# Query projections in one earlier slot, the query rows' transfers ahead of the left half's, and a reordered prologue, in a macaron block on one core

## The reference

```python
x = x + 0.5 * ffn(layernorm(x))     # ffn: fft, matmul with a complex w, real part of ifft, + bias
x = x + attn(layernorm(x))          # 16 heads of 8, q/k/v from the LEFT 128 features, then Wo and bo
x = x + 0.5 * ffn(layernorm(x))
# attn: softmax(q @ k.T / 4) @ v per head
```

## Time and profile before

| | us |
|---|---|
| median of 3 runs | 317.19 |
| lowest, highest | 316.79, 319.31 |
| profiled execution, its own time | 320.35 |
| its span | 318.5 |
| busy share of the span: PE, ACT, DVE, POOL | 94%, 81%, 60%, 31% |
| DMA, mean | 157 GB/s |
| granted TensorE clock | 1.000 of full speed |

### The profile page before, as it was taken

One profiled execution on the slowest core, in us unless ns is written; L12 is line 12 of the kernel. 1 busy time (PEld: TensorE's weight loads), 2 busy tenths in 40 slices (PEclk: granted clock), 3 DMA queues, 4 the chain that ended last, 5 costly groups with the idle time before them and its releaser, 6 DMA issues.

```text
span 318.5 us, 8826 instructions
## 1 busy us (share of the span) xinstructions
PE 298.2 (94%) x3445; PEld 113.4 (36%) x3449; DVE 189.6 (60%) x550; ACT 259.3 (81%) x287; POOL 97.7 (31%) x112
## 2 busy tenths in 40 slices
PE   8888899899999999999997999899998999998985
PEld 5644333233333333333332333233332333222333
DVE  1687535758775778477863778367854653360264
ACT  2215989998998989898996989798998999999921
POOL 6734701043604251404504251403500340034014
PEclk9999999999999999999999999999999999999999
DMA  7835572146456364825474363625461564112102
GB/s 202 312 134 196 204 285 115 58 160 240 138 184 221 134 199 141 290 105 200 133 224 176 134 201 117 184 101 199 136 203 66 185 214 165 38 68 66 36 33 68
DMA packets 26564, 49.86 MB, mean 157 GB/s; under 512 B 2065, under 2 KB 14737, under 8 KB 24721
## 3 DMA queue, kind: packets, MB, share of 16 engines
q1 hardware_dynamic: 25824, 48.78, 44.4%
q10 hardware_dynamic: 688, 0.40, 0.7%
HBM read 31.34 MB, written 17.83 MB: 154 GB/s over the span
## 4 chain that ended last, share of the span: by engine, by line
PE 66%; DMA 11%; DVE 10%; issue 6%; ACT 5%; POOL 1%; SPq 1%; PEldq 0%; ACTq 0%; DVEq 0%
PE misc L715 24%; PE ot L823 24%; PE scores L795 12%; DMA QS<-q_scr 9%; ACT probs L665 5%; DMA left_scr<-left_blocks 3%; PE scores L682 2%; DVE left_blocks L963 2%; PE scores L715 1%; PE scores L689 1%; DVE kp L982 1%; DVE lh L954 1%; DVE kp L980 1%; DVE stats L936 1%; DVE VS L1027 1%
## 5 line engine op out<-in xcount | busy, mean ns | idle before, releaser
L665 ACT ACTIVATE probs<-scores 128x1024 f32<-128x1024 f32 x256 | 243.9, 1029 | 25.6 <-PE scores L795 22.7
L823 PE MATMUL ot<-probs,VS 128*32 128x512 f32 x1024 | 134.4, 594 | 3.9 <-ACT probs L665 2.9
L795 PE MATMUL scores<-QS,KS 32*128 32x512 f32 x512 | 64.8, 495 | 5.7 <-DMA QS<-q_scr 5.0
L795 PEld LDWEIGHTS scores<-QS,KS 32*128 32x128 f32 x512 | 24.5, 181 | 112.8 <-ACT probs L665 100.3
L1014 DVE SCALAR_TENSOR_TENSOR x_out<-misc,rstd,x_out 128x256 f32<-128x256 f32 x28 | 13.6, 484 | 48.2 <-PE misc L715 44.8
L823 PEld LDWEIGHTS ot<-probs,VS 128*32 128x32 f32 x1024 | 30.8, 109 | 28.0 <-ACT probs L665 7.1
L558 POOL TENSOR_TENSOR x_out<-x,half_bias 128x512 f32<-128x512 f32 x7 | 9.0, 1290 | 92.4 <-DVE x L1009 92.4
L543 POOL TENSOR_SCALAR veps<-mv 128x4 f32<-128x4 f32 (+1 forms) x25 | 5.7, 227 | 96.4 <-DVE mv L943 96.4
L715 PE MATMUL misc<-half_ffn,xT 128*32 128x256 f32 x448 | 33.1, 387 | 0.0
L715 PE MATMUL misc<-half_ffn,xT_in 128*32 128x256 f32 x400 | 27.9, 385 | 1.8 <-DVE half_ffn L1185 1.3
L545 POOL TENSOR_TENSOR rstd<-veps,power 128x4 f32<-128x4 f32 (+1 forms) x25 | 25.2, 1008 | 2.1
(11 more groups left out here) (126 smaller groups left out, 259.3 us busy)
## 6 DMA issues: line engine op xcount, KB each, us to landing
KS<-k_scr SPq DMA_DIRECT2D x14, 512.0 KB, 4.5
QS<-q_scr SPq DMA_DIRECT2D x14, 512.0 KB, 4.5
x_in<-x SPq DMA_DIRECT2D x8, 512.0 KB, 6.4
xT_in<-x_t SPq DMA_DIRECT2D x8, 512.0 KB, 7.3
k_scr<-kp SPq DMA_DIRECT2D x8, 512.0 KB, 2.8
q_scr<-qp SPq DMA_DIRECT2D x8, 512.0 KB, 3.7
x_scr<-x_blocks SPq DMA_DIRECT2D x7, 512.0 KB, 3.5
xT<-x_scr SPq DMA_DIRECT2D x7, 512.0 KB, 4.5
```

Source lines behind the costliest of these rows:

```text
L665: nc.scalar.activation(probs[u % PRING][:, :, :], scores[u % SRING][:, :, :], ACT.Exp, scale=SCORE_SCALE).then_inc(exp_done, 1)
L795: last = mm(scores[(u + j // 2) % SRING][:, j % 2, :], KS[b % 2][rows, slot, kt * P:(kt + 1) * P].bitcast(F32R), QS[b % 2][rows, slot, :]. ...
L823: last = mm(ot[COL * j:COL * (j + 1), :], VS[b % 2][:, kt, h, :], probs[(u + j // 2) % PRING][:, j % 2, :], start=s % 8 == 0, stop=s % 8 == 7)
```

## The change

In `STEADY` both QT halves move to slot 6 (one left, one right), F1_3 moves from 6 to 7, and V_0 and V_1 stand apart in 8 and 9 (before: QT_0 in 7, QT_1 in 8, both V in 9). DVE's `left_half` goes from slots 8 and 9 to 9 and 10, and ACT's square of the queries from quad 10 to 9. `BEGIN` is mixed anew: KT and QT halves share slots with F1 parts, and V comes in 11 and 12. SP issues both query row loads straight behind the query store, ahead of the left half's two transfers, and the x loads behind an output store. In the prologue all of batch 0's statistics come behind the second fold, POOL's rstd ahead of its bias adds, and batch 1's statistics behind the guard's maxima.

```diff
 STEADY = ...
-          6: [("F1_3a", 2, LEFT), ("F1_3", 2, LEFT)], 7: [("QT_0", 1, LEFT)], 8: [("QT_1", 1, LEFT)],
-          9: [("V_0", 1, RIGHT), ("V_1", 1, LEFT)], 10: ...
+          6: [("QT_0", 1, LEFT), ("QT_1", 1, RIGHT)], 7: [("F1_3a", 2, LEFT), ("F1_3", 2, LEFT)],
+          8: [("V_0", 1, RIGHT)], 9: [("V_1", 1, LEFT)], 10: ...
-BEGIN = {1: [("LT", 1, LEFT)], 2: [("KT_0", 1, LEFT), ("KT_1", 1, RIGHT)], 3: [("QT_0", 1, LEFT), ("QT_1", 1, RIGHT)],
-         4: [("F1_0a", 2, LEFT), ("F1_0", 2, LEFT)], 5: [("F1_1a", 2, LEFT)], 6: [("F1_1", 2, LEFT), ("F1_2a", 2, RIGHT)],
-         7: [("F1_2", 2, RIGHT)], 8: [("F1_3a", 2, LEFT), ("F1_3", 2, LEFT)], 9: [("V_0", 1, RIGHT)],
-         10: [("V_1", 1, LEFT), ("N", 1, RIGHT)]}
+BEGIN = {1: [("LT", 1, LEFT)], 2: [("KT_0", 1, RIGHT), ("F1_0a", 2, LEFT)], 3: [("F1_0", 2, LEFT), ("KT_1", 1, RIGHT)],
+         4: [("F1_1a", 2, LEFT)], 5: [("F1_1", 2, LEFT), ("QT_0", 1, RIGHT)], 6: [("F1_2a", 2, LEFT)],
+         7: [("F1_2", 2, LEFT), ("QT_1", 1, RIGHT)], 8: [("F1_3a", 2, LEFT), ("F1_3", 2, LEFT)],
+         10: [("N", 1, RIGHT)], 11: [("V_0", 1, RIGHT)], 12: [("V_1", 1, LEFT)]}
...
             for it in range(1, B):
+                if it >= 2:
+                    store_out(it - 2, 1)
                 if it + 3 < B:
                     load_x(it + 3)
-                if it >= 2:
-                    store_out(it - 2, 1)
...
                     q_out(it + 1)
+                    q_in(it + 1)
                 if it + 2 < B:
                     left_through(it + 2)
-                if it + 1 < B:
-                    q_in(it + 1, slice(0, 1))
-                if it + 2 < B:
                     leftT_in(it + 2)
-                if it + 1 < B:
-                    q_in(it + 1, slice(1, None))
                 store_out(it - 1, 0)
...
+            rstd_of(0, 1)
             pool.wait_ge(bias_set, 1)
             pool.wait_ge(x_loaded[0], 16)
-            add_row(x1[0], x_in[0], half_bias, early_biased, slice(0, 2))
-            rstd_of(0, 1)
+            add_row(x1[0], x_in[0], half_bias, early_biased, slice(0, 1))
+            add_row(x1[0], x_in[0], half_bias, early_biased, slice(1, 2))
...
-                    if s == (2 * (8 if it == B - 2 else 10) if it else 2 * 7):
+                    if s == (2 * 9 if it else 2 * 10):
                         square(qp, sq_q, qp_step, it + 1)
...
-            norm0_stats(0, range(0, 2))
...
-            norm0_stats(0, range(2, T))
+            norm0_stats(0)
...
-            for s in range(T, T + 6):
-                run_jobs(PROLOGUE, s)
+            run_jobs(PROLOGUE, T)
+            for t in range(T):
+                evacuate(f"F1_{t}", 1)
+            run_jobs(PROLOGUE, 2 * T + 1)
+            run_jobs(PROLOGUE, 2 * T + 2)
             dve.wait_ge(row_ready, 1)
             nc.vector.tensor_copy(KS[0][:, 0, :].bitcast(F32R), row_banks[0]).then_inc(first_k_set, 1)
-            run_jobs(PROLOGUE, T + 6)
-            run_jobs(PROLOGUE, T + 7)
+            run_jobs(PROLOGUE, 2 * T + 3)
+            dve.wait_ge(evacuated, evac_count(f"F1_{T - 1}", 1))
+            for t in range(T):
+                norm_stats(1, x1[1], t, t == T - 1)
+            norm_moments(1, 2)
             guard(0)
...
-                        if s == (8 if it else 10):
+                        if s == (9 if it else 10):
                             left_half(it + 2, range(0, 2))
-                        if s == (9 if it else 11):
+                        if s == (10 if it else 11):
                             left_half(it + 2, range(2, T))
                             turn_left(it + 2)
```

More of the change, by code:

```diff
@@ L71 @@
           4: [("F1_1a", 2, LEFT), ("F1_1", 2, LEFT)], 5: [("F1_2a", 2, LEFT), ("F1_2", 2, LEFT)],
-          6: [("F1_3a", 2, LEFT), ("F1_3", 2, LEFT)], 7: [("QT_0", 1, LEFT)], 8: [("QT_1", 1, LEFT)],
-          9: [("V_0", 1, RIGHT), ("V_1", 1, LEFT)], 10: [("N", 1, RIGHT), ("F2_0a", -1, LEFT)], 11: [("F2_0", -1, LEFT)],
+          6: [("QT_0", 1, LEFT), ("QT_1", 1, RIGHT)], 7: [("F1_3a", 2, LEFT), ("F1_3", 2, LEFT)],
+          8: [("V_0", 1, RIGHT)], 9: [("V_1", 1, LEFT)], 10: [("N", 1, RIGHT), ("F2_0a", -1, LEFT)], 11: [("F2_0", -1, LEFT)],
           12: [("F2_1a", -1, LEFT), ("F2_1", -1, LEFT)], 13: [("F2_2a", -1, LEFT), ("F2_2", -1, LEFT)],
           14: [("F2_3a", -1, LEFT)], 15: [("F2_3", -1, LEFT)]}
-BEGIN = {1: [("LT", 1, LEFT)], 2: [("KT_0", 1, LEFT), ("KT_1", 1, RIGHT)], 3: [("QT_0", 1, LEFT), ("QT_1", 1, RIGHT)],
-         4: [("F1_0a", 2, LEFT), ("F1_0", 2, LEFT)], 5: [("F1_1a", 2, LEFT)], 6: [("F1_1", 2, LEFT), ("F1_2a", 2, RIGHT)],
-         7: [("F1_2", 2, RIGHT)], 8: [("F1_3a", 2, LEFT), ("F1_3", 2, LEFT)], 9: [("V_0", 1, RIGHT)],
-         10: [("V_1", 1, LEFT), ("N", 1, RIGHT)]}
+BEGIN = {1: [("LT", 1, LEFT)], 2: [("KT_0", 1, RIGHT), ("F1_0a", 2, LEFT)], 3: [("F1_0", 2, LEFT), ("KT_1", 1, RIGHT)],
+         4: [("F1_1a", 2, LEFT)], 5: [("F1_1", 2, LEFT), ("QT_0", 1, RIGHT)], 6: [("F1_2a", 2, LEFT)],
+         7: [("F1_2", 2, LEFT), ("QT_1", 1, RIGHT)], 8: [("F1_3a", 2, LEFT), ("F1_3", 2, LEFT)],
+         10: [("N", 1, RIGHT)], 11: [("V_0", 1, RIGHT)], 12: [("V_1", 1, LEFT)]}
 LATE = {0: [("KT_0", 1, RIGHT)], 1: [("KT_1", 1, RIGHT)],
@@ L100, in slots_of @@
         ahead = [(f"F1_{t}", 2) for t in range(T)]
-        jobs = [(f"F1_{t}", 1) for t in range(T)] + [("LT", 1)] + ahead[0:3] + [("KT", 1), ("QT", 1)] + ahead[3:4] + [("N", 1)]
+        jobs = [(f"F1_{t}", 1) for t in range(T)] + [("LT", 1)] + ahead + [("KT", 1), ("QT", 1), ("N", 1)]
         return {s: [(name, d, LEFT)] for s, (name, d) in enumerate(jobs)}
@@ L624, in _ @@
                 nc.scalar.copy(copy[:, :, :], half_bank(bank)).then_inc(ffn_copied, 1)
-            act.wait_ge(bias_loaded, 16)
-            nc.scalar.mul(half_bias[:, :], bias_raw[:, :], 0.5).then_inc(bias_set, 1)
             for piece, bank, copy in ((5, scores[0][:, 0], even[2]), (6, scores[0][:, 1], odd)):
@@ L629, in _ @@
                 nc.scalar.mul(copy[:, :, :], half_bank(bank), 0.5 / E).then_inc(ffn_copied, 1)
+            act.wait_ge(bias_loaded, 16)
+            nc.scalar.mul(half_bias[:, :], bias_raw[:, :], 0.5).then_inc(bias_set, 1)
             act.wait_ge(pick_loaded, 16)
@@ L1002, in evacuate @@
                     if b == 0 and i < 2:
-                        dve.wait_ge(early_biased, 1)
+                        dve.wait_ge(early_biased, i + 1)
                     else:
```

## The result

The changed kernel takes 322.51 us (median of 4 runs, 322.08 to 322.53) beside 318.12 for the kernel before (4 runs, 316.79 to 319.31): ratio 1.0135, 95% interval 1.0101 to 1.0168, so it is slower, by 1.35%. The ratios of the experiments leave out runs more than 1.5% above the fastest of their kernel, which are runs of the kernel before alone. Forecast were 324.2 and a range of 320.4 to 326.0. The profiled execution took 322.08, span 320.3, against 320.35 and 318.5.

The account below looks back on a forecast made before the run. PE, busy 94% of the span, was taken as the bound, each of its waits counting whole. Against the profiled 320.35, -5.0 + 10.3 - 0.4 - 0.3 = +4.6 gave 325.0; the median forecast was 324.2, range 320.4 to 326.0.

Parts of the forecast that it names:

- The forecast case: Whole kernel: query rows in time, three new DVE waits per steady iteration cost more; median 324.2 us; chance 58%.
- 0.8 had been taken off for another reason: Sum 325.0 lowered to 324.2: profiled execution was 3.2 above the median, perhaps partly something every profiled execution pays.
- four instructions in slot 6: Steady slot 6: DVE empties both QT halves before slot 7's job, which starts 1.97 after v, not 1.41: +0.56.
- F1_3 ahead of the transpose of `ot`: Steady slot 7: F1_3 and statistics precede the transpose, so slot 8's value products wait, 2.56 in place of 1.88: +0.68.
- left half behind the guard's chain: Steady slot 10: F2_0 is emptied behind chain and left half, so slot 12's job starts at 4.09, not 3.27: +0.82.
- waits that went, ends of five iterations: Score products of a new batch no longer wait for query rows, as the query store leaves earlier: -5.0 us.
- iteration 0: Two four-instruction slots lose 0.56 each; new waits of some 0.17 in slots 3 and 5, 0.35 in 7: -0.4.
- prologue: POOL's rstd and bias adds 0.2 to 0.3 later, N's chain 0.85 earlier: -0.3, from -0.85 to +0.3.
- the rival on the faster side: Half slots: ACT, not PE, paces PE, so PE makes up its waits; 313.7 to 314.5 us; chance 6%.
- the rival of late rows: Query rows or left half still late at one or two places, 1 to 2 us: 326 to 328; chance 8%.
- fear of the dummies: Prologue: dummy products queued on PE might hold its guard read and ACT's first exponential, so -0.3 and not -0.85.
- The rival by which the profiled execution was slow throughout: Profiled execution was slow everywhere, not in its waits; same cost on a median of 317.19: 321.8 us; chance 15%.

Follow-up runs that it names:

- e5: Changed kernel with DVE's whole left half and its block transpose in slot 9, ahead of the guard's chain: 318.77 us, ratio 1.0046 to the kernel before.
- e6: Changed kernel with the transpose of `ot` in steady slot 7 between the emptying of F1_3 and its statistics: 319.26 us, ratio 1.0063 to the kernel before.
- e7: Changed kernel with left half whole in slot 9 and the transpose of `ot` ahead of F1_3's statistics: 315.78 us, ratio 0.9945 to the kernel before.
- e3: Changed kernel with the steady table, left half slots and square slot of before; SP's order, iteration 0 and prologue as changed: 314.16 us, ratio 0.9876.
- e1: Kernel before, with SP issuing both query row loads behind the query store, ahead of the left half's two transfers: 314.41 us, ratio 0.9893.
- e10: Kernel before with only iteration 0 and the prologue changed; steady table and SP's order as before: 316.25 us, ratio 0.9946.
- e4: Changed kernel with steady table, left half slots, square slot and iteration 0's table of before; SP's order and prologue as changed: 313.98 us, ratio 0.9908.
- e2: Kernel before, with the x loads behind the second output store of an iteration: 317.54 us, ratio 0.998.
- e9: Changed kernel with steady table, left half slots, square slot and early prologue of before; SP's order, iteration 0 and late prologue as changed: 313.95 us, ratio 0.9887.
- e11: Kernel with old steady table and early prologue, otherwise as changed, but left half's store ahead of both row loads, its load behind: 313.21 us, ratio 0.9839.
- e8: Changed kernel with ten dummy products in place of five between the first score products and PE's read of the guard: 322.66 us, a single execution.

## Why the prediction was right, and where it was off

The forecast case was the one that came: the rows in time, three new waits of DVE in each steady iteration, and these the dearer. It put the median 1.7 us too high and the sum for the profiled execution 2.9 too high (325.0 against 322.1). That the median came out nearer than the sum is luck: 0.8 had been taken off for another reason, and the changed kernel's profiled execution lies 0.4 below its median. By its terms:

| term | forecast | measured |
|---|---|---|
| four instructions in slot 6, each iteration | 0.56 | 0.57 |
| F1_3 ahead of the transpose of `ot` | 0.68 | 0.58 |
| left half behind the guard's chain | 0.82 | 0.71 |
| the three, in five iterations | +10.3 | +9.3 |
| waits that went, ends of five iterations | -5.0 | 3.55 - 9.3 = -5.8 |
| iteration 0 | -0.4 | -0.66 |
| prologue | -0.3 | -0.97, of which -0.41 by the change |
| iteration 6 | 0 | -0.12 |

*The new waits.* e5 takes away 0.70, e6 0.58, e7 1.28, and e3 all three, 1.87 (36.30 to 34.43). The chains were right and slightly too long. The statistics ended 1.81 after v as forecast, but the transpose of `ot` began 0.08 before the end of their record and not 0.02, and took 0.69 and not 0.72. In slot 10 the guard's chain took 1.56 and not 1.59, the transpose of the left half let the next instruction start after 1.04 and not 1.08, and F2_0 took 0.44 and not 0.48. No slot of 1.86 in a steady iteration shrank behind a wait, so PE made up nothing, and the rival on the faster side is out.

*The query rows.* The forecast has the mechanism of SP's queue right (e1, e10), and e1 and e3 add what it didn't weigh: it never asked whether slot 6 was needed for it, and it isn't. The -5.8 holds the 5.0 of the list and two things that the list leaves out. One is some 0.3 by which the slots' distances exceed the waits listed. The other is 0.50 at the end of iteration 1, which is no wait for rows: the rows were in, and slot 15's value products themselves took 1.54 in place of 1.04, with a gap of PE's weight loads in their midst that the trace puts down to nothing. Its cause is open, and e1 and e3 don't have it. The late left half, a part of the rival of late rows, didn't come in the changed kernel, because the left half's store leaves there long after the loads: at 127.92, 7.7 us behind them. In e3, where it leaves right behind them, it did.

*Iteration 0.* The two slots with four instructions are rid of their 0.57 each, and slots 3 and 5 wait 0.17 each, as forecast. Slot 7 costs 0.23 (from its v to the next it takes 2.53 in place of 2.30) and not 0.35. e4 has 0.60 for the whole table. The -0.12 of iteration 6 wasn't in the sum; there ACT's square of the queries also moves, from quad 8 to 9.

*The prologue.* The term was wrong in three parts that I had mixed. To tell them apart, count from PE's first F1 job, which begins at 12.60 before and 12.04 after.

The early part's new order costs 0.56, not 0.2 to 0.3: the left half's rstd starts 6.25 after F1 in place of 5.69. All traces with the new early part have 6.24 to 6.26, all with the old one (before, e1, e2, e9, e11) 5.69. What I had too small is the delay of POOL's first rstd: against F1 it starts 0.91 later (1.12 ahead of it before, 0.21 ahead after) and not 0.6 to 0.7. The bias adds behind it took 5.1 us, nearly the 5.0 that I had summed.

The guard's chain ends 15.57 after F1 in e9 and 16.81 before, 1.24 earlier, where I had 0.85. ACT's start gained 1.00 of it (17.15 in place of 18.15), and I had taken only part of 0.85 for fear of the dummies. The Trainium skill's sentence on the sequencer ("TensorE: Matmul & The Clock Gate", "Step-by-step: what each phase is for") speaks against that fear, and e8 agrees with it: 17.77 against 17.73 with twice the dummies. The net gain of the reordering in the changed kernel is 0.41 (first value products 20.23 after F1 before, 19.82 after).

The other 0.56 of the 0.97 is no effect of the change: PE's second piece of the fold (its weight loads) started at 5.69 in place of 6.25 in that execution, F1 at 12.04 in place of 12.60, both 6.35 apart. Seven other traces here with the same early part have F1 anywhere from 11.92 to 12.87, 6.34 to 6.37 behind that piece. Why the piece started earlier stays open: its 256 KB of weights landed only 0.1 us sooner (3.9 us after their issue in place of 4.0).

*From the profiled execution to the median.* I took most of the 3.2 us between them for waits that go away anyway, and the runs fit that: the changed kernel's four runs lie within 0.45 us, while those of the kernel before spread over 2.5. The rival by which the profiled execution was slow throughout would have given 321.8, nearer to the result than my number, but by the wrong way: the remaining difference is in the terms above.

## What to carry to other kernels

Where a slot's work on the bounding engine waits for a serial helper to empty the slot before, count the helper's instructions between two hand-overs: a job that is moved to be early for one consumer (a DMA) can make others late, here three times an iteration. A transfer that is late needs first a look at what stands ahead of it in its queue, a wait of another transfer above all; here an edit of order (e1) took away all waits for the rows without moving any compute. And behind such an edit look at what now comes right behind large transfers: a small store behind two large loads took 4.9 to 6.7 us in place of 2.1.

## What was not expected of the hardware

A 256 KB store to memory, issued right behind two loads of 512 KB each, needed 4.9 to 6.7 us (e1, e3, e9) until its reader could be issued. Issued just ahead of them it needed 2.1 (e11), and 7.7 us behind them 2.1 too (the changed kernel).

ACT's first exponential, which needs PE's read of a value and a branch, follows 1.3 to 1.7 us after the value is written (29.41 to 30.75 before, 28.15 to 29.77 after, 28.04 to 29.69 in e8), whether five or ten products are queued ahead of it. What sets it between these two isn't settled. With the new order of the chain the first score products may be the limit: ACT starts 1.35 to 1.42 after they do (after, e3, e8, e9, e11), in the kernel before 2.36.
